# A rotation attention stage: wide weights loaded later, the first pair finished by VectorE, the spread moved ahead of the next pair's sums

## The reference

```python
# end of layer 0: x1 is normed; two expert rows per token are chosen
    moe_out = jnp.sum(sel * top_gates[..., None], axis=2)
    return _layer_norm(x1 + moe_out, ln2_w, ln2_b)
...
    x = x + _L0_ffn_ref(_layernorm(x), ...)
# rotation attention, B=32 batches, H=16 heads of HD=16, nq=8
def _L1_attn_ref(x, wq, bq, wk, bk, wv, bv, wo, bo, w1, b1, w2, b2, hadamard, rot):
    Q, K, V = x @ wq + bq, x @ wk + bk, x @ wv + bv          # (B, S, H, HD)
    prep = lambda t: jnp.tanh(t @ w1 + b1) @ w2 + b2         # 16 -> 256 -> 16
    q1, k1 = (qp[..., :nq] + 1j * qp[..., nq:]) @ Hc, ...    # Hadamard
    # R mixes batches 2i and 2i+1 for i < 4; the other batches stay
    qe = jnp.real(jnp.einsum('hcb,bshn->cshn', R, q1)); ke = ...
    qq, kk = jnp.sum(qe ** 2, -1), jnp.sum(ke ** 2, -1)
    s = qq[:, :, None, :] * kk[:, None, :, :]
    attn = jax.nn.softmax(s / s, axis=2)
    out = jnp.einsum('bijh,bjhd->bihd', attn, V)
    return out @ wo + bo
...
x = x + _L1_attn_ref(_layernorm(x), ...)
```

## Time and profile before

| what | us |
|---|---|
| median of 3 runs | 3866.34 |
| profiled execution | 3859.17 |
| its span | 3857.3 |
| PE busy | 3590.2 (93%) |
| opening of the stage, from its first instruction to the first `make_rows` of TensorE | 31.4 (1433.8 to 1465.2) |
| from there to the stage's last addition | 420.0 (1465.2 to 1885.2) |

### The profile page before, as it was taken

One profiled execution on the slowest core, in us unless ns is written; L12 is line 12 of the kernel. 1 busy time (PEld: TensorE's weight loads), 2 busy tenths in 40 slices (PEclk: granted clock), 3 DMA queues, 4 the chain that ended last, 5 costly groups with the idle time before them and its releaser, 6 DMA issues. The chain is left out here.

```text
span 3857.3 us, 70844 instructions
## 1 busy us (share of the span) xinstructions
PE 3590.2 (93%) x25500; PEld 2491.7 (65%) x25501; DVE 1935.2 (50%) x6159; ACT 1616.0 (42%) x3427; POOL 1577.0 (41%) x2148
## 2 busy tenths in 40 slices
PE   8998799998999776899799999999999989999998
PEld 6776455555777663444366666666666659899986
DVE  4554666664677644565355545555555546311113
ACT  4553455554665404577344444444444431111111
POOL 1000333333577504555055555555555547200015
PEclk9999999998999888999899999999999989999998
DMA  9301111110000072000100000000000001699962
GB/s 285 154 0 26 39 36 37 37 25 12 6 20 19 25 209 46 16 20 14 34 7 13 7 7 7 12 8 7 7 7 13 1 1 50 226 325 325 327 230 85
DMA packets 111410, 262.38 MB, mean 68 GB/s; under 512 B 24003, under 2 KB 70240, under 8 KB 95840
## 3 DMA queue, kind: packets, MB, share of 16 engines
q1 hardware_dynamic: 90208, 224.70, 18.2%
q0 software_dynamic: 16384, 26.29, 2.5%
q10 hardware_dynamic: 4608, 8.39, 0.6%
HBM read 196.61 MB, written 62.65 MB: 67 GB/s over the span
## 5 line engine op out<-in xcount | busy, mean ns | idle before, releaser
L2286 POOL TENSOR_SCALAR wide_probs<-wide_probs,wide_inverse 100x361 f32<-100x361 f32 x512 | 607.4, 1198 | 0.1
L2467 ACT ACTIVATE wide_probs<-wide_probs,wide_least 100x361 f32<-100x361 f32 x512 | 300.9, 589 | 626.8 <-DVE wide_least L2533 626.8
L2533 DVE CUSTOM_DVE_ANT_0 wide_probs<-banks,wide_bias 100x361 f32<-100x361 f32 x512 | 251.7, 529 | 123.0 <-issue 123.0
L2284 POOL TENSOR_TENSOR wide_hold_pool<-eps 100x1 f32<-100x1 f32 x256 | 51.0, 199 | 577.7 <-DVE wide_inverse L2539 576.3
L1976 ACT ACTIVATE rot_h<-banks,w_rot_b 128x800 f32<-128x800 f32 x256 | 223.6, 924 | 114.4 <-PE banks L1850 110.7
L2342 PE MATMUL banks<-w_wide_v,wide_c 64*120 64x512 f32 (+1 forms) x1152 | 263.5, 589 | 2.5 <-DVE wide_v L2519 1.8
L2336 PE MATMUL banks<-wide_c,w_wide_k 64*128 64x361 f32 x1536 | 255.4, 464 | 3.1 <-DVE wide_kT L2516 2.3
L2378 PEld LDWEIGHTS banks<-ident,wide_probs 100*120 100x120 f32 (+1 forms) x1536 | 158.5, 172 | 149.6 <-issue 119.3
L2364 PE MATMUL banks<-wide_kT,wide_qT 64*100 64x361 f32 x1024 | 220.8, 508 | 1.7 <-issue 1.7
L2881 PEld LDWEIGHTS banks<-tiles_xT,tiles_w 128*128 128x128 f32 x1824 | 212.5, 192 | 4.5 <-issue 1.6
L2881 PE MATMUL banks<-tiles_xT,tiles_w 128*128 128x128 f32 x1824 | 213.0, 275 | 1.2 <-DVE tiles_xT L3127 1.2
(11 more groups left out here) (451 smaller groups left out, 7789.7 us busy)
## 6 DMA issues: line engine op xcount, KB each, us to landing
tiles_w<-in_moe_w SPq DMA_DIRECT2D x114, 1024.0 KB, 5.1
slots<-zeros SPq DMA_DIRECT2D x58, 512.0 KB, 5.7
cross_c<-in_ctxT SPq DMA_DIRECT2D x32, 270.8 KB, 4.4
wide_c<-in_ctxT SPq DMA_DIRECT2D x32, 270.8 KB, 4.0
mix_kT<-slots SPq DMA_DIRECT2D x32, 256.0 KB, 4.1
slots<-mix_kT ACTq DMA_DIRECT2D x32, 256.0 KB, 3.9
tiles_rows<-slots SPq DMA_DIRECT2D x57, 128.0 KB, 4.8
slots<-tiles_out SPq DMA_DIRECT2D x57, 128.0 KB, 5.0
```

The lines of the kernel that those rows point to most:

```text
L2286: last = nc.gpsimd.tensor_scalar(t.probs[:, i % RING, j, :], t.probs[:, i % RING, j, :], t.inverse[:, i % RING, j:j + 1], None, ALU.mult)
L2467: last = nc.scalar.activation(t.probs[:, i % RING, j, :], t.probs[:, i % RING, j, :], ACT.Exp, bias=t.least[:, i % RING, j:j + 1], scale=-1.0,
L2533: last = nc.vector.tensor_tensor_reduce(t.probs[:, i % RING, j, :], scores(j), t.bias[:, :], -1.0, LARGEST, ALU.add, ALU.min, t.least[:, i ...
```

## The change

Six edits, all in `rotation_phase`. SyncE waits for four additions to x (`s.stored`, two pairs of two lanes) ahead of its loads. `v.sum` gets two sets, and `combine` waits for the pair two back. GpSimd's opening order is changed, with the second pair's gathers in two halves. The first pair's scale, shift and addition to x are done by VectorE. VectorE's opening does `apply(FIRST)` ahead of `combine(SECOND)`. In `run`, VectorE's `weigh(before)` moves from behind `add_rows_up` to the place right behind `apply(after)`, and `add_rows_up(after)` moves ahead of `second_norm(following)`.

```diff
-        v = buffers(nc, ctx, "rot_moe", got=[S, SETS, LANES, 2, D], sum=[S, LANES, D], hold=[S, SETS], seen=[S, SETS])
+        v = buffers(nc, ctx, "rot_moe", got=[S, SETS, LANES, 2, D], sum=[S, SETS, LANES, D], hold=[S, SETS], seen=[S, SETS])
         @block.sync
         def _(sp):
+            sp.wait_ge(s.stored, 2 * LANES)
             for sem, dst, src in g.loads:
                 sp.dma_start(dst, src).then_inc(sem, 16)
...
-            def gather(pr):
-                pool.wait_ge(s.copied, pr[2])
-                nc.gpsimd.tensor_tensor(v.hold[:, pr[0]:pr[0] + 1], g.eps[0:S, :], g.eps[0:S, :], ALU.add).then_inc(s.held, 1)
-                for lane in range(LANES):
+            def gather(pr, lanes=range(LANES)):
+                if 0 in lanes:
+                    pool.wait_ge(s.copied, pr[2])
+                    nc.gpsimd.tensor_tensor(v.hold[:, pr[0]:pr[0] + 1], g.eps[0:S, :], g.eps[0:S, :], ALU.add).then_inc(s.held, 1)
+                for lane in lanes:
...
-            gather(FIRST)
-            gather(SECOND)
             nc.gpsimd.memset(t.imag[:, P - NQ:P], 0.0).then_inc(s.zeroed, 1)
             pool.wait_ge(g.loaded.rot, g.total.rot)
+            gather(FIRST)
+            gather(SECOND, [0])
             roots(m0, FIRST)
-            add_rows(FIRST)
+            gather(SECOND, [1])
+            roots(m1, FIRST)
+            add_bias(FIRST)
             roots(m0, SECOND)
-            roots(m1, FIRST)
             add_rows(SECOND)
             gather(THIRD)
-            add_bias(FIRST)
             pairs(pool, run)
...
             def combine(pr):
                 dve.wait_ge(gathered[pr[0]], pr[5])
-                if not (isinstance(pr[1], int) and pr[1] == 0):
-                    dve.wait_ge(s.stored, pr[1] * LANES if isinstance(pr[1], int) else pr[3][0][1])
+                if not (isinstance(pr[1], int) and pr[1] < SETS):
+                    stored = (pr[1] - 1) * LANES
+                    dve.wait_ge(s.stored, stored if isinstance(pr[1], int) else dve.snap(stored))
...
                 if after:
                     apply(after)
+                if before:
+                    weigh(before)
                 if following:
                     combine(following)
+                if after:
+                    add_rows_up(after)
                 if third:
                     copy_slots(third)
                 if following:
                     second_norm(following)
-                if after:
-                    add_rows_up(after)
-                if before:
-                    weigh(before)
                 if pr[4]:
                     turn_by(pr, 1)
...
             combine(FIRST)
             second_norm(FIRST)
-            combine(SECOND)
+            for lane, b, n in FIRST[3]:
+                dve.wait_ge(s.out, n)
+                nc.vector.tensor_tensor(v.sum[:, 0, lane, :], v.sum[:, 0, lane, :], w.ln2_w[:, :], ALU.mult).then_inc(s.out_scaled, 1)
+            for lane, b, n in FIRST[3]:
+                dve.wait_ge(s.out_scaled, n)
+                nc.vector.tensor_tensor(v.sum[:, 0, lane, :], v.sum[:, 0, lane, :], w.ln2_b[:, :], ALU.add).then_inc(s.out_shifted, 1)
+            for lane, b, n in FIRST[3]:
+                dve.wait_ge(s.out_shifted, n)
+                nc.vector.tensor_tensor(g.x[:, b, :], g.x[:, b, :], v.sum[:, 0, lane, :], ALU.add).then_inc(s.stored, 1)
             stats(FIRST)
             copy_slots(THIRD)
+            apply(FIRST)
+            combine(SECOND)
+            add_rows_up(FIRST)
             second_norm(SECOND)
-            apply(FIRST)
-            add_rows_up(FIRST)
             keep_mean(FIRST)
             pairs(dve, run)
```

More of the change, by code:

```diff
@@ L1755, in add_rows @@
                     pool.wait_ge(s.out, n)
-                    nc.gpsimd.tensor_tensor(v.sum[:, lane, :], v.sum[:, lane, :], w.ln2_w[:, :], ALU.mult).then_inc(s.out_scaled, 1)
+                    nc.gpsimd.tensor_tensor(v.sum[:, pr[0], lane, :], v.sum[:, pr[0], lane, :], w.ln2_w[:, :], ALU.mult).then_inc(s.out_scaled, 1)
                 for lane, b, n in pr[3]:
                     pool.wait_ge(s.out_scaled, n)
-                    nc.gpsimd.tensor_tensor(v.sum[:, lane, :], v.sum[:, lane, :], w.ln2_b[:, :], ALU.add).then_inc(s.out_shifted, 1)
+                    nc.gpsimd.tensor_tensor(v.sum[:, pr[0], lane, :], v.sum[:, pr[0], lane, :], w.ln2_b[:, :], ALU.add).then_inc(s.out_shifted, 1)
                 for lane, b, n in pr[3]:
@@ L1762, in add_rows @@
                     pool.wait_ge(s.out_shifted, n)
-                    nc.gpsimd.tensor_tensor(g.x[:, row, :], g.x[:, row, :], v.sum[:, lane, :], ALU.add).then_inc(s.stored, 1)
+                    nc.gpsimd.tensor_tensor(g.x[:, row, :], g.x[:, row, :], v.sum[:, pr[0], lane, :], ALU.add).then_inc(s.stored, 1)
             def add_bias(pr):
```

8 lines of the change are left out of this document (4 added, 4 removed).

## The result

| | before | after |
|---|---|---|
| median of runs, us | 3864.2 (3861.97 to 3866.84, 4 runs) | 3821.42 (3819.41 to 3829.01, 4 runs) |
| ratio to before, 95% interval | | 0.9893 (0.9876 to 0.991) |
| profiled execution: span, us | 3857.3 | 3827.2 |
| the rotation stage in it, us | 451.3 | 415.0 |

The change makes the kernel 1.07% faster, 41.3 us by the ratio (35 to 48). 3827 was predicted (39.5 us), with 3816 to 3846 as the range. The profiled execution of after took 3829.01, the longest of its four, so the stage is compared with the stage, and the whole by the ratio. Outside the stage the two profiled executions differ by 6.2 us the other way (3857.3 - 451.3 against 3827.2 - 415.0), in code that the change doesn't touch.

A forecast was written before the change was run, and what follows sets the result against it. A chain of other engines and transfers was taken to bound the opening, TensorE nearly the rest. Gains 13.0 + 23.9 - 2.4 + 5.0 = 39.5 us took 3866.34 to 3826.8, say 3827; range 3816 to 3846.

The forecast's parts named there:

- The opening, 13.0: Start of the rotation stage: first y at 1452.1 in place of 1465.12, a gain of 13.0 us.
- the low end for the landing: First pair's gathers: without the wide loads beside them, combine can start at 1441.5; the other end was 1449.1.
- The third pair, "covered with 2.8 to spare": Third pair's gathers meet the wide loads, yet `ybar` comes at 1479.9, before TensorE wants it at 1482.7.
- The 13 waits, 23.9: Turns: the earlier spread removes all 13 waits of `project` for the weighted heads, gaining 23.9 us.
- The loop, 22.1, loses 2.4: Turns: a GpSimd and VectorE loop of 22.1 us exceeds TensorE's 21.75 by 0.37, costing 2.4 us over nine turns.
- No collisions: Turns: GpSimd's addition to x takes the short 1.40 us, not 2.08, beside VectorE's addition from PSUM.
- the 6 us: Turns: further loss if GpSimd's addition and VectorE's PSUM addition held each other up, loop 22.8; left out of the sum.
- The clock, 5.0: Turns: three of four half-clock drops behind waits stay away, gaining 5.0 us, bounds 0 and 6.5.
- The loop at 24.1: Rival, turns: the GpSimd loop sets the pace at 24.1 us, gain only 21.8, time 3844.5; chance 0.18.
- Third gathers waiting for all the loads: Rival, opening: third pair's gathers wait until about 1489, `ybar` 9.7 us late, time 3836.5; chance 0.09.
- First gathers landing no sooner: Rival, opening: first gathers land no sooner without the loads, 7.6 us less gain, time 3834.4; chance 0.07.
- Slower, by gathers of 2.2 each: Rival, turns: VectorE's work stretches GpSimd's gather issue, loop 27.7 us, 10.7 slower, time 3877; chance 0.02.

The follow-up runs named there:

- loads_now: The changed kernel with SyncE's wait ahead of the wide loads taken out; ratio to before 0.9906, stage 422.0 us.
- wait_alone: The kernel before, with only SyncE's wide loads made to wait for the second pair's stores; ratio to before 1.0004, stage 451.4 us.
- memset_alone: The kernel before, with only the memset moved ahead of the gathers; ratio to before 1.0011, stage 451.5 us.
- loads_third: The changed kernel, with the wide loads waiting until the third pair's gathers have landed; ratio to before 0.9876, stage 409.8 us.
- gpsimd_more: The changed kernel, with two extra additions of 0.70 us on GpSimd in each turn; ratio to before 0.9913, stage 427.0 us.
- spread_behind: The changed kernel, with the weighted spread put back behind the following pair's norm; ratio to before 0.9972, stage 444.8 us.
- again: The changed kernel unchanged, rerun as control; ratio to before 0.9904, stage 413.3 us.
- rows_shared: The changed kernel, with loads waiting for the third pair's gathers and the following pair's addition to x on VectorE; ratio to before 0.9899, stage 411.7 us.
- rows_gpsimd: The changed kernel, with the first pair's three additions of rows back on GpSimd; ratio to before 0.9908, stage 419.5 us.
- spread_alone: The kernel before, with only the weighted spread moved ahead of the following pair's combine; ratio to before 0.9931, stage 424.5 us.

## Why the prediction was right, step by step

- *The opening, 13.0.* Measured 12.7. Combine was due 7.6 into the stage (1441.5 less 1433.87) and came at 8.3: the first gather was issued 0.3 later (1.2 into the stage, where 0.9 was kept from before), and the fourth landed 2.0 after its issue and not 1.7. The six additions took 2.1 and not 2.5. The choice of the low end for the landing was right: loads_now puts it 9.2 later. That the memset and the loads are one edit in effect stood in the prediction only as two waits 0.38 apart; wait_alone and memset_alone show it.
- *The third pair, "covered with 2.8 to spare".* This step failed, by 1.0 us. Combine came 43.8 into the stage, where 42.6 was predicted, VectorE waited 8.1 where some 7 were, and I followed only `ybar`. The rotation of the vectors (L2105) stands behind the same combine in VectorE's order, and `last_layer` wants it before anything wants `ybar`: 1.41 of waiting, 26.4 for the turn in place of 25.4. loads_third takes the wait away and has 25.4. With a short first turn the step costs more: 2.9 in gpsimd_more (28.3).
- *The 13 waits, 23.9.* All gone, and back with 23.8 in spread_behind.
- *The loop, 22.1, loses 2.4.* The loop is 21.98 where it runs undisturbed (the gathers of again start 21.98 apart turn after turn), TensorE's own turn 21.82 and not 21.75. Ten turns take 219.3 in again, 1.1 over ten times 21.82, and this is the loop: `make_rows` starts 0.1 to 0.2 late, behind y, in six of them. gpsimd_more shows that the loop is there and that it is level with TensorE; rows_shared that without it each turn is TensorE's own. So the loop is shown, and its price was over-estimated. In after the ten turns take 220.5, 2.3 over, and that this is the 2.4 of the prediction is luck: none of it is a wait for y. Four of its turns are 22.2 to 22.7 long, and in each of them y is there 0.5 to 0.95 ahead of `make_rows`. The longest, with the end of the turn:

```profile
1709.95 0.91 PE L1881 MATMUL banks<-rot_squares,rot_sum 128*128 128x400 f32 x2 [0.16 <-issue]
1710.67 1.75 ACT L1978 ACTIVATE rot_h<-banks,w_rot_b 128x800 f32<-128x800 f32 x2 [0.86 <-PE banks L1852]
...
1711.12 0.57 POOL L91 TENSOR_TENSOR rot_ln_rstd<-rot_ln_vareps,neg_half 100x1 f32<-100x1 f32 x1
1711.45 0.57 DVE L2118 TENSOR_TENSOR rot_least<-banks,rot_k_least 128x400 f32<-128x400 f32 x1 [1.99 <-PE banks L1881]
...
1711.74 0.95 PE L1852 MATMUL banks<-rot_q,rot_w 32*128 32x400 f32 x8 [0.88 <-ACT rot_h L1978]
...
1712.42 0.73 DVE L96 TENSOR_SCALAR rot_y<-x,rot_ln_meanvar,rot_ln_rstd 100x256 f32 x2
...
1714.11 0.56 PE L1818 MATMUL banks<-ident,rot_y 100*128 100x100 f32 x4
```

  TensorE stands idle for 0.16 ahead of its second product for the norms (L1881) and for 0.88 behind it, for ScalarE's tanh; in again it idles for 0.24 there in all. The four turns have 0.6 to 1.0 of it, and the long ones of rows_gpsimd (up to 23.06, hence its 222.8 for ten) 0.6 to 1.4. The granted clock is 1.00 throughout. ScalarE starts its tanh 0.9 behind the matmuls that it waits for, and VectorE its product (L2118) 0.6, where again has less than 0.1 for either; ends of matmuls are modelled in the profile, so it doesn't tell which engine was late, or why. That stays open. Both profiles with such turns come from series in which the kernel before takes 3864 and 3865. The seven others with the spread moved come from those with 3843 and 3844 and have none; six of them take 218.2 to 219.3 for the ten turns, and gpsimd_more has its longer loop. The sum of the loop also left out that y's norm stands on VectorE behind the product L2118, which waits for TensorE: here the first root is ready at 1711.69, and y comes at 1712.42.
- *No collisions.* GpSimd's addition to x took 1.41 and not 2.08 or more, as the prediction took it, since VectorE does nothing with two SBUF operands then. Its addition from PSUM (one SBUF input) takes 0.75 beside GpSimd's 1.42 and holds up neither. By the rule of the Trainium skill that the prediction cited (SBUF — State Buffer, "Who interferes with whom") the 6 us stay out, and the trace agrees. The other half of this rule of the Trainium skill, that two SBUF inputs on VectorE do contend with a GpSimd instruction that reads SBUF, shows as well: in the opening GpSimd's bias and VectorE's combine take 1.83 and 1.81 beside each other, in place of 1.40 and 0.88 alone. The Trainium skill's rule on gather descriptors and two-port instructions (SBUF — State Buffer, "SBUF: two separate sides") would, by the prediction's estimate, have held the opening by up to 3.8. The gathers beside the tables took 1.08, 1.02, 1.09 and 1.01 each, against 1.10 and three times 1.01 in the turns, so here it cost 0.1 at most.
- *The clock, 5.0.* All four short drops of before are gone, 6.5, the upper bound. But the first turn of after is 2.7 longer than of before, at half clock for nearly all of it, and no term held that.
- *Sum.* In the stages: 12.7 - 2.7 - 1.0 + 10.8 + 16.5 = 36.3 in after, and 38.0 in again, against 39.5. In the prediction's terms the last two of after are 23.9 of waits and 6.5 of clock, less 2.3 of long turns and 0.8 for TensorE's own turn, thirteen times 0.07 longer than reckoned. So two terms that weren't there (2.7 and 1.0) and the 0.8 took away 4.5, and the clock gave 1.5 more than forecast. By the ratio 41.3 for after and 36.9 for again (0.0096 x 3843), so the 39.5 stands 1.5 to 3.2 above the stage's gain and inside either interval. That the time came out 5.6 under 3827 is due to no step of the sum: the median of before, against which the forecast was set, went from 3866.3 to 3864.2 with one more run, and the rest lies outside the stage; that it is scatter is likely (the four runs of after are 3819 to 3829), and not shown.
- *The rivals.* The loop at 24.1: no, 21.98. Third gathers waiting for all the loads (combine 55 into the stage): no, 43.8. First gathers landing no sooner: no. Slower, by gathers of 2.2 each in place of 1.3, idle time between them included: four took 5.04 from the first issue to the end of the last, 1.3 each.

## What to carry to other kernels

When two waits end close together, an edit to one of them measures nothing; try both before dropping either. When a wait is taken off the engine that sets the pace, add up the loop through the other engines from their rows: here it stood 0.2 us above TensorE's own turn, and the next 1.4 us of work put into it cost 1.4 a turn. A total that agrees with the forecast isn't the mechanism yet: look whether the engine waits for what the loop delivers. And where an in-order engine is made to wait, follow every instruction queued behind the wait to the first one that somebody needs, not only the one you have in mind.

## What was not expected of the hardware

- Four gathers of 100 rows land 2.0 us after the last issue with the queues empty. Beside some 27 us of plain loads the first pair's landed 15.2 to 17.6 into the stage in three profiles that waited for them (in spread_alone by 14.8), in place of 8.3, and the third pair's 43.8 in place of 35.6 at the latest.
- With the same code ahead of it, TensorE's clock came back to 2.4 GHz within the first turn in some executions (18.9 us) and only at its end in others (21.7). That is 2.8 us between kernels that don't differ up to there, as much as the wait taken out in loads_third is worth at most.
- Chips differ by 22 us in the kernel before (3865 against 3843), and the difference lies outside this stage: span less stage is 3407 to 3412 in the four profiles of the one series, and 3384 to 3390 in the eight of the two others.
